# The window mask written into the score banks by ScalarE instead of TensorE, and two buffers for the output projection's weights

## The reference

```python
# per layer l of 6; x is [16, 256, 128], 16 heads of 64, window w = 32
x = attn_layer(shift_tokens(x), Wqkv[l], q_scale[l], k_scale[l], Wo[l]) + x
x = ffn_layer(shift_tokens(x), ln_g[l], ln_b[l], W1[l], b1[l], W2[l], b2[l]) + x

# in attn_layer: q, k normalised, scaled and rotated; then, window by window,
# 32 queries against 64 keys (the window before and this one):
mask = (it < jb) | (it > jb + w) | (jb == -1)
sim = einsum('bhwie,bhwje->bhwij', bq, bk2) * 8.0
sim = where(mask, -finfo.max, sim)
attn = softmax(sim, -1)
out = einsum('bhwij,bhwje->bhwie', attn, bv2)
return out.reshape(b, n, 1024) @ Wo
```

## Time and profile before

| what | value |
|---|---|
| device time, median of 3 runs (lowest, highest) | 3678.64 us (3673.33, 3685.43) |
| span of the profiled execution (its device time is not given apart) | 3676.2 us |
| PE busy | 3451.3 us, 94% |
| PEld busy | 2721.5 us, 74% |
| DVE busy | 2806.8 us, 76% |
| ACT busy | 2365.2 us, 64% |
| POOL busy | 2815.1 us, 77% |
| mean granted clock of TensorE | 0.973 of full speed |

### The profile page before, as it was taken

The page is one execution under the profiler, slowest core; times in us unless marked ns, Lnnn a source line. Parts: engine busy times, 40 slices in busy tenths (PEclk is TensorE's granted clock), DMA queues, the critical chain, the costliest instruction groups (busy, mean ns, idle before and its releaser), DMA issues.

```text
span 3676.2 us, 148973 instructions
## 1 busy us (share of the span) xinstructions
PE 3451.3 (94%) x64612; PEld 2721.5 (74%) x64612; DVE 2806.8 (76%) x4876; ACT 2365.2 (64%) x4307; POOL 2815.1 (77%) x3470
## 2 busy tenths in 40 slices
PE   3799986999999999999999999999999999999997
PEld 2566544788877888777888778877788887788775
DVE  3477666888887888878888878887788888788863
ACT  3333223677766777777777677776677777777663
POOL 1355546998887888878888888888788888888772
PEclk9799997999999999999999999999999999999999
DMA  3333212111111111211111121112111111112110
GB/s 100 98 97 93 87 31 58 47 43 39 46 47 49 40 41 44 51 44 42 45 38 46 44 52 39 42 43 52 40 46 42 40 45 50 44 40 50 36 43 24
DMA packets 126733, 183.48 MB, mean 50 GB/s; under 512 B 29824, under 2 KB 61440, under 8 KB 126080
## 3 DMA queue, kind: packets, MB, share of 16 engines
q1 hardware_dynamic: 119232, 146.15, 15.8%
q0 software_dynamic: 6848, 27.80, 2.5%
HBM read 59.01 MB, written 14.16 MB: 20 GB/s over the span
## 4 chain that ended last, share of the span: by engine, by line
PE 85%; POOL 5%; DVE 3%; issue 3%; ACT 1%; DMA 1%; SPq 0%; ACTq 0%; POOLq 0%; DVEq 0%
PE bank L550 22%; PE bank L622 10%; PE bank L633 9%; PE bank L595 7%; PE bank L560 5%; PE bank L570 4%; PE bank L606 4%; PE bank L696 3%; PE bank L674 3%; PE bank L685 3%; PE bank L582 2%; PE bank L465 1%; PE bank L525 1%; PE bank L642 1%; PE bank L504 1%
## 5 line engine op out<-in xcount | busy, mean ns | idle before, releaser
L550 PE MATMUL bank<-wqkv,xs 128*128 128x512 f32 x3456 | 1061.5, 423 | 17.1 <-DVE m L1029 13.1
L1684 POOL TENSOR_TENSOR m<-m 128x512 f32<-128x512 f32 x576 | 728.7, 1285 | 45.2 <-DVE m L1029 42.6
L550 PEld LDWEIGHTS bank<-wqkv,xs 128*128 128x128 f32 x3456 | 582.8, 191 | 146.0 <-issue 56.9
L1029 DVE TENSOR_TENSOR m<-bank,tab 128x512 f32<-128x512 f32 x768 | 521.5, 679 | 0.7 <-POOL m L1684 0.3
L1358 ACT ACTIVATE sq<-bank 128x512 f32<-128x512 f32 x768 | 458.5, 597 | 98.1 <-PE bank L550 54.2
L1692 POOL TENSOR_TENSOR S<-S,nw 128x1024 f32<-128x1024 f32 x192 | 383.3, 1996 | 168.0 <-DVE S L1060 168.0
L1040 DVE TENSOR_REDUCE ss<-sq 128x8 f32<-128x512 f32 x768 | 504.9, 674 | 0.0
L1700 POOL TENSOR_TENSOR S<-S,rs 128x512 f32<-128x512 f32 x384 | 411.0, 1091 | 69.7 <-DVE rs L1074 67.9
L622 PEld LDWEIGHTS bank<-P,big 64*64 64x64 f32 x24576 | 379.6, 135 | 79.8 <-issue 72.3
L1027 DVE TENSOR_TENSOR m<-bank,tab 128x512 f32<-128x512 f32 x576 | 392.1, 681 | 57.4 <-ACT sq L1358 41.9
L633 PE MATMUL bank<-OT,wo 128*128 128x128 f32 x3072 | 389.9, 282 | 40.8 <-ACT P L1397 27.6
(11 more groups left out here) (232 smaller groups left out, 6457.1 us busy)
## 6 DMA issues: line engine op xcount, KB each, us to landing
big<-vst SPq DMA_DIRECT2D x1536, 64.0 KB
stage<-in_wqkv SPq DMA_DIRECT2D x36, 256.0 KB, 3.0
tab<-in_tab SPq DMA_DIRECT2D x48, 128.0 KB, 2.2
xsort<-big SPq DMA_DIRECT2D x4, 960.0 KB, 8.6
big<-xsort SPq DMA_DIRECT2D x12, 256.0 KB, 4.5
ysort<-big SPq DMA_DIRECT2D x12, 256.0 KB, 3.6
wo<-in_wo SPq DMA_DIRECT2D x6, 512.0 KB, 3.7
big<-in_x SPq DMA_DIRECT2D x8, 256.0 KB, 3.4
```

What stands on the lines that cost most here:

```text
L550: m = eng.matmul(pb[:, :], xt[a], wqkv[:, z, 512 * part:512 * part + 512], start=(n == 0), stop=(n == 2))
L1029: eng.tensor_tensor(m2[:, s3, :].rearrange("p (h s d) -> p h s d", s=2, d=DH // 2), pw, sn.rearrange("p (s d) -> p s d", s=2).unsqueeze(1) ...
L1684: eng.tensor_tensor(turned(g, part), turned(g, part), m2[:, part % 2, :], ALU.add).then_inc(s["g_add"], 1)
```

## The change

Two edits. First, `mask` goes from PE's program, with its tables `mkb` and `idb` and the five ACT instructions that made them; ACT gets `masked(n - 2)` in front of `v_out(n, 0)`: two ACTIVATE instructions that copy the fp32 mask, repeated eight times along the row, from SBUF into the banks 4 and 5. They wait for the same count of `v_sm`. `sim` waits for them (`a_mk`) and adds its products on top as before. Second, `wo` has two halves, one for odd and one for even layers; the weights of layer `l + 1` are loaded in pass `32 l + 6`, a layer ahead.

```diff
-        wo = sb("wo", [P, 8, 128])
+        wo = sb("wo", [P, 2, 8, 128])
-        mkb = sb("mkb", [2 * W, 3, 512], BF16)
-        idb = sb("idb", [2 * W, P], BF16)
...
-        wb = {"wv": flat(wo[:, :, :]), "perm": ffn[:, 0:1024], "wo": flat(tab[:, 0, 0:2, :])}
+        wb = {"wv": flat(wo[:, 1, :, :]), "perm": ffn[:, 0:1024], "wo": flat(tab[:, 0, 0:2, :])}
...
-                    if n % 32 == 5 and n > 32:
-                        q.wait_ge("p_wo", n - 5)
-                        eng.dma_start(wo[:, :, :], wo_d[l]).then_inc(s["d_wo"], 16)
+                    if n % 32 == 6 and l + 1 < DEPTH:
+                        q.wait_ge("p_wo", n - 6)
+                        eng.dma_start(wo[:, (l + 1) % 2, :, :], wo_d[l + 1]).then_inc(s["d_wo"], 16)
...
-            def mask(g):
-                if not 0 <= g < NG:
-                    return
-                c = g // 4 % NC
-                pe.wait_ge("a_mb", 5)
-                for par in range(2):
-                    pe.wait_ge("v_sm", 2 * (g - 1) + par + 1)
-                    rows = slice(W * par, W * par + W)
-                    eng.matmul(bank[4 + par][:, :], idb[rows, :], mkb[rows, 0 if c == 0 else 1 + c % 2, :], start=True, stop=False)
-
             def sim(g):
...
                 pe.wait_ge("g_zero", 1)
+                pe.wait_ge("a_mk", 2 * g + 2)
...
-                    m = eng.matmul(pb[:, 0:128], wo[:, r, :], OT[:, g % 2, r, :], start=(r == 0), stop=(r == 7))
+                    m = eng.matmul(pb[:, 0:128], wo[:, g // 32 % 2, r, :], OT[:, g % 2, r, :], start=(r == 0), stop=(r == 7))
...
                 turn_k(n - 2, 1)
-                mask(n - 2)
                 proj(n, 5)
...
-            msk = kc[0:2 * W, KC["mask"]].rearrange("p (v k) -> p v k", v=3)
-            for v in range(3):
-                eng.activation(mkb[:, v, :].rearrange("p (r k) -> p r k", r=8), msk[:, v, :].unsqueeze(1).to_broadcast([2 * W, 8, 64]), ACT.Copy,
-                               scale=1.0, bias=0.0).then_inc(s["a_mb"], 1)
-            for n in range(2):
-                rows = slice(W * n, W * n + W)
-                eng.activation(idb[rows, :].rearrange("p (b t) -> p b t", b=4), kc[rows, rows].unsqueeze(1).to_broadcast([W, 4, W]), ACT.Copy,
-                               scale=1.0, bias=0.0).then_inc(s["a_mb"], 1)
...
+            def masked(g):
+
+                if not 0 <= g < NG:
+                    return
+                c = g // 4 % NC
+                v = KC["mask"].start + 64 * (0 if c == 0 else 1 + c % 2)
+                ac.wait_ge("v_rb", NC)
+                ac.wait_ge("v_tq", NC)
+                for par in range(2):
+                    ac.wait_ge("v_sm", 2 * (g - 1) + par + 1)
+                    eng.activation(bank[4 + par][:, :].rearrange("p (r k) -> p r k", r=8), kc[:, v:v + 64].unsqueeze(1).to_broadcast([P, 8, 64]),
+                                   ACT.Copy, scale=1.0, bias=0.0).then_inc(s["a_mk"], 1)
...
                     end_centred(u - 5)
+                masked(n - 2)
                 v_out(n, 0)
```

More of the change, by code:

```diff
@@ L216, in program @@
             p_proj p_tq p_tk p_sim p_pt p_av p_wo p_lnc p_lnv p_lnb p_fg p_fa p_fw p_ec p_ev p_eb
-            a_sq a_vst a_tq a_tk a_exp a_p2 a_oev a_xf a_hi a_halo a_mb a_x2s a_halo2 a_ln a_xn a_xh a_w1 a_gelu a_e a_w
+            a_sq a_vst a_tq a_tk a_exp a_p2 a_oev a_xf a_hi a_halo a_mk a_x2s a_halo2 a_ln a_xn a_xh a_w1 a_gelu a_e a_w
             v_w1 v_xl v_k v_ss v_sm v_max v_sum v_rec2 v_res v_lo v_ln v_xn v_h v_X v_back v_e v_out v_w
@@ L320, in _ @@
             eng.dma_start(tab[:, 0, :, :], tab_d[0]).then_inc(s["d_tab0"], 16)
-            eng.dma_start(wo[:, :, :], wo_d[0]).then_inc(s["d_wo"], 16)
+            eng.dma_start(wo[:, 0, :, :], wo_d[0]).then_inc(s["d_wo"], 16)
             eng.dma_start(w1, w1_d[0]).then_inc(s["d_ffn"], 16)
@@ L595, in sim @@
                             m = eng.matmul(bank[4 + par][32 * b:32 * b + 32, 64 * r:64 * r + 64], qT[rows, g % 2, r, 32 * b:32 * b + 32],
-                                           kT[rows, r, :, 4 * i + b, :], start=False, stop=(r == 7))
+                                           kT[rows, r, :, 4 * i + b, :], start=False, stop=(r == 7), skip_group_check=True)
                 m.then_inc(s["p_sim"], 1)
```

## The result

| | before | after |
|---|---|---|
| median | 3675.98 us | 3637.06 us |
| runs | 3672.07 to 3685.43 (4) | 3635.34 to 3639.89 (4) |
| ratio | | 0.989, 95% interval 0.9874 to 0.9905 |
| profiled span | 3676.2 us | 3633.5 us |

The kernel became 39 us faster. The prediction was 3602 us, a gain of 77 us: the time lies inside the range of 3563 to 3650, but outside the forecast's own range of 3589 to 3618. Half of the gain is missing, and most of what follows is about where it went. The two traced executions differ by 42.7 us; the rest of the difference to 39 lies in which executions were traced. Of the ten executions of `swap`, further down, one took 7215 us and stands in no ratio; all the others of every kernel are in one state.

The account below looks back on a forecast made before the run. PE was taken to bound the kernel, with nobody keeping it waiting. Mask passes 55, `wo` 19.3 and the start 2.2 made 76.6 us, off the median of 3678.6: 3602 us, range 3563 to 3650, own range 3589 to 3618.

Parts of the forecast that it names:

- What bounds the kernel: Transformer loop: PE is busy all 61 us of a stretch, so work leaving its program shortens the kernel.
- What is late next: At `gate`, `variance` and `sim`: PE then waits for ACT's second key-turn copy, limiting the gain to 1.28 us a unit.
- The copies on ScalarE: Ahead of `v_out`: two mask copies of 0.6 us each, hidden by ACT's idle time and 0.32 us of room.
- Two buffers for `wo`: In front of L633: five waits, 13.2 us, go, and full clock gives 6.1 us; together 19.3 us.
- Rival 2: In front of L633: the `wo` stall hides other lateness, so its 19.3 us are lost; 3621 us, chance 0.10.
- The start: Ahead of the recurrence's first copy: ACT's five setup instructions go, saving 2.2 us, bounds 0 and 2.2.
- The sum: Whole kernel: 55 + 19.3 + 2.2 = 76.6 us, taken off the median of 3678.6 us, gives 3602 us.
- Rival 3: Transformer passes: POOL or DVE take the mask's gain; 3657 us, chance 0.09.
- Rival 1: At PE's wait for turned keys: the hand-over doesn't bind, as the copy comes earlier too; full 94 us, 3563 us, chance 0.08.
- Rival 4: At the second L1384: ACT's writes into PSUM are dear, 1.29 us each, delaying 2.26 us a unit; 3700 us, chance 0.08.

Follow-up runs that it names:

- swap: Kernel after with both key turns ahead of projection parts 3 and 5 on PE, and ACT's order to match; ratio 0.9971 to the kernel before.
- no_copies: Kernel after without ScalarE's 384 copies of the mask, so without the mask; ratio 0.9944 to the kernel before.
- wo_narrow: Kernel before with two `wo` buffers, and the mask kept as 3 x 64 columns read eight times over; ratio 0.9949 to the kernel before.
- split: Kernel after with the score products' wait for the second half of turned keys moved from row 0 to row 4; ratio 0.9801 to the kernel before.
- shift: Kernel after with 64 one-column fp32 products (256 PE instructions) ahead of the transformer loop; ratio 0.9929 to the kernel before.

## Why the prediction was half right

- *What bounds the kernel* ("Nobody keeps PE waiting there, so what leaves PE's program shortens the kernel, as long as nothing that PE waits for comes due instead"): this step failed. I listed engines and data as what could come due. What came due was TensorE's own program, which no row of engine waits names. It could be read before: the 5.9 us of "issue" inside the score products, 11 times, sat in the same list as the 13.2 us of the earlier trace rows, and I went past it as small.
- *What is late next*: right. Forecast 1.28 us a unit, measured 1.17 in undisturbed passes (51.5 us in place of 56.3). The 0.14 us for `gate` and `variance` was right in size, but not as the delay that I took it for: the start is 0.05 us behind the copy, and the products then take 0.07 and 0.11 us longer, which makes 0.12 and 0.16. `q4 = 0` fell short with 0.30 of 0.41, by the 0.10 us that the score products lose there and that are gone in `no_copies`.
- *The copies on ScalarE*: right, 0.597 us against 0.6, and no wait; but they were put at nothing for TensorE, and `no_copies` shows 0.10 us a pass with `q4 = 0`. The Trainium skill's "ScalarE: Activation LUTs", section "What ACT_TABLE_LOAD costs", makes it 0.61 us, an estimate from its figures, and the trace agrees. Its remark that PSUM is the faster destination can't be settled here: the nearest copy from SBUF to SBUF (L1417, which writes another type) has a median of 630 ns, and L1338, a square of the same size from PSUM to SBUF, a mean of 597.
```profile
L1338 ACT ACTIVATE sq<-bank 128x512 f32<-128x512 f32 x768 | 458.9, 597 | 92.4 <-PE bank L548 54.5
```

- *Two buffers for `wo`*: right. Forecast 19.3 us, 22.5 in the first pair of traces, 19 by `wo_narrow`. Rival 2 fell: the trace of the kernel after has no wait left there.
- *The start*: too high. The recurrence's first copy starts at 7.98 in place of 9.06, as the table load that had been hidden behind the wait for constants now stands in front of it: 1.1 us of 2.2.
- *The sum*: 76.6 us had the right terms and one missing, -28 us for the fetch. With it the sum is 48.6, 3630 us, against the 3637 measured. Of the difference 4.8 us are the passes, 2.1 the value products and 1.1 the start, and the `wo` passes gave 3.2 more; that leaves 43.8, and the two traces differ by 42.7. The median of the kernel before, 3679 in the forecast, also came out at 3676 over four runs. That 3637 lies inside the stated range is luck: the range reached that far for rivals 2 and 3, which did not happen.
- *Rivals 1, 3 and 4*: none of them. The hand-over binds; POOL and DVE keep TensorE waiting 3 us more than before in all (33.5 us against 30.6, and 66.2 against 66.3); writes into PSUM aren't dear. Rival 3, that the mask's gain goes elsewhere, was the nearest in spirit, but 17 of the 55 us arrived. (Rival 4's 2.26 us a unit leaves `q4 = 2` out, for which no row was read.)

## What to carry over

In a kernel bound by TensorE, look at the "issue" waits inside runs of small products and ask where they fall in the program: a run of some 100 products can use up its instructions faster than the next 256 arrive, and the transfer starts late when the sequencer has to stand at a wait just in front of the run. Then removing work in front of the run, or tightening that wait, moves the stall in; letting the first half of the run go with the part of its data that is there early brings it out again. Count instructions, not products: whether such a test moves anything depends on the number modulo 256, and one fp32 product of one column was four in these traces.

## What I had not expected of the hardware

- The program itself is a stream that can run dry: 1.2 to 1.9 us of stall per block's edge in the wrong place, 40 to 56 us a run in the kernel after and most of its variants, 28 in `split`, 12 before. A transfer takes 1.0 us in the records, but 2.2 to 3.0 us pass from its start to the next product.
- Adding work can leave the stalls where they were or move them all: the 64 fp32 products of `shift` (128 matmuls in the trace, 0.213 us each) left the same 15 units stalled (and one more); 32 moved every one.
- A hand-over from ScalarE to TensorE is 0.05 us in front of `sim`, `gate` and `variance` alike, but the products behind it can be slower than without a wait: by 0.07 us for `gate`, by 0.11 for `variance`, by nothing for `sim` with `q4 = 2`.
- Instructions of ScalarE that TensorE doesn't wait for can still cost it time: 0.10 us per 128 score products with `q4 = 0`, gone when the mask's copies are left out. The cause is open.
